# Channel mix's first buffers laid over attention's idle slots, its weights and first chunk prepared in attention's last groups, inverse sums by batch

## The reference

```python
x = x + attention(layernorm(x))          # 16 heads of 32, rotated q and k, softmax, then @ Wo + bo
# channel mix, on y = layernorm(x), y_prev = y one token earlier (zeros in front)
xr = mu_r * y + (1 - mu_r) * y_prev
xk = mu_k * y + (1 - mu_k) * y_prev
r = sigmoid(xr @ W_r.T)
k = square(relu(xk @ W_k.T))
x = x + r * (k @ W_v.T)
```

## Time and profile before

| | us |
|---|---|
| median of the runs | 3142.26 |
| lowest and highest run | 3140.79, 3144.47 |
| the profiled execution | 3138.19 |
| its span, first to last instruction | 3136.1 |
| TensorE busy | 3022.8 |
| GpSimd busy | 2093.0 |
| VectorE busy | 2239.5 |
| ScalarE busy | 1487.5 |

### The profile page before, as it was taken

The page is one execution under the profiler, slowest core; times in us unless marked ns, Lnnn a source line. Parts: engine busy times, 40 slices in busy tenths (PEclk is TensorE's granted clock), DMA queues, the critical chain, the costliest instruction groups (busy, mean ns, idle before and its releaser), DMA issues. The chain is left out here.

```text
span 3136.1 us, 42811 instructions
## 1 busy us (share of the span) xinstructions
PE 3022.8 (96%) x15468; PEld 2016.3 (64%) x15468; DVE 2239.5 (71%) x3351; ACT 1487.5 (47%) x2714; POOL 2093.0 (67%) x715
## 2 busy tenths in 40 slices
PE   7999999989999999999999999999967999999998
PEld 4888888855555555555555555555525777877776
DVE  4555556568777777777777777777628778678784
ACT  1222222226666666666666666666742223223232
POOL 0211112118999999999999999999944665666663
PEclk8999999989999999999999999999988999999999
DMA  3554545664656464655656464646243323313311
GB/s 105 173 183 167 177 168 177 188 152 107 137 115 145 99 146 107 139 119 126 132 123 140 108 145 98 149 109 135 52 125 87 108 62 99 107 54 107 107 54 41
DMA packets 188922, 381.78 MB, mean 122 GB/s; under 512 B 17088, under 2 KB 53088, under 8 KB 180704
## 3 DMA queue, kind: packets, MB, share of 16 engines
q1 hardware_dynamic: 179696, 313.70, 36.3%
q0 software_dynamic: 9072, 66.06, 10.3%
HBM read 194.59 MB, written 118.49 MB: 100 GB/s over the span
## 5 line engine op out<-in xcount | busy, mean ns | idle before, releaser
L278 DVE TENSOR_REDUCE part_max<-ps_m 128x1 f32<-128x512 f32 x1984 | 1213.8, 681 | 333.9 <-PE ps_m L262 333.0
L950 POOL TENSOR_TENSOR pairs<-probs 128x2048 f32<-128x2048 f32 x255 | 1179.8, 4632 | 144.6 <-ACT probs L923 131.8
L923 ACT ACTIVATE probs<-ps_s 128x512 f32<-128x512 f32 x2048 | 1036.6, 623 | 292.7 <-PE ps_s L815 276.8
L262 PE MATMUL ps_m<-k_stack,q_stack 96*128 96x512 f32 x1984 | 820.3, 415 | 15.0 <-DVE neg_max L275 8.2
L815 PE MATMUL ps_s<-q_stack,k_stack 97*128 97x512 f32 x2048 | 817.1, 402 | 5.6 <-PEq L311 3.6
L262 PEld LDWEIGHTS ps_m<-k_stack,q_stack 96*128 96x128 f32 x1984 | 376.7, 190 | 287.7 <-DVE part_max L278 136.7
L828 PE MATMUL ps_o<-probs,v_tiles 128*32 128x512 f32 x4096 | 495.6, 602 | 0.0
L815 PEld LDWEIGHTS ps_s<-q_stack,k_stack 97*128 97x128 f32 x2048 | 388.0, 190 | 130.0 <-ACT probs L923 21.2
L541 POOL TENSOR_TENSOR ln_rstd<-ln_rstd,ln_minus_half 128x4 f32<-128x4 f32 x16 | 16.1, 1009 | 415.9 <-DVE ln_rstd L584 415.9
L957 POOL TENSOR_TENSOR pairs<-pairs 128x2048 f32<-128x2048 f32 x63 | 288.4, 4578 | 4.9
L828 PEld LDWEIGHTS ps_o<-probs,v_tiles 128*32 128x32 f32 x4096 | 107.3, 109 | 234.5 <-issue 176.6
(11 more groups left out here) (180 smaller groups left out, 4809.8 us busy)
## 6 DMA issues: line engine op xcount, KB each, us to landing
pairs<-pairs POOLq DMA_DIRECT2D x63, 1024.0 KB, 8.5
q_stack<-q_hi_scratch SPq DMA_DIRECT2D x128, 256.0 KB, 6.2
k_stack<-k_hi_scratch SPq DMA_DIRECT2D x64, 512.0 KB, 10.7
x_in<-in_x SPq DMA_DIRECT2D x16, 1024.0 KB, 5.4
q_hi_scratch<-st_hi SPq DMA_DIRECT2D x64, 256.0 KB, 2.2
q_lo_scratch<-st_lo SPq DMA_DIRECT2D x64, 256.0 KB, 2.5
k_hi_scratch<-st_hi SPq DMA_DIRECT2D x64, 256.0 KB, 2.4
k_lo_scratch<-st_lo SPq DMA_DIRECT2D x64, 256.0 KB, 2.6
```

Of the source, the lines that this page charges most:

```text
L262: nc.tensor.matmul(bank[:, :], att["q"][r][0:ROWS, half, h, q * P:(q + 1) * P], att["k"][r][0:ROWS, h, kc * CH:(kc + 1) * CH], start=True, ...
L278: nc.vector.reduce_max(part_max[:, half, j, kc:kc + 1], bank[:, :], AX).then_inc(att["m_read"], 1)
L923: nc.scalar.activation(probs[:, (r * UNITS + u) % PR, x // HG, x % HG, :], ps_s[place(u * UT + x) % SR][:, :], ACT.Exp, scale=SCALE).then_ ...
L950: nc.gpsimd.tensor_tensor(pairs[:, w, :, :], probs[:, (r * UNITS + u) % PR, 0, :, :], probs[:, (r * UNITS + u) % PR, 1, :, :], ALU.add).th ...
```

## The change

- Attention's three slots keep their sizes, but the buffers of slots 0 and 2 are now laid over buffers that the mix keeps: in slot 0 `o_hi`, `o_lo`, `w_o`'s low part, `x_in`, `bo` and a quarter of `gate`; in slot 2 `w_o`'s high part, the low parts of w_k, w_r, w_v and `relu`. The raw weights are loaded to where their low parts will be made in place. `neg_max` has one half instead of two, with a wait on the copy of the other half before it is written.
- In group 30 SP loads w_k, w_r, w_v, mu_r and mu_k. In group 31 it loads w_o, the first chunk's outputs and inverse sums, bo and the first x. In the last group VectorE divides the chunk, and w_o and the chunk are split by ScalarE and VectorE; ScalarE's two casts stand before its last `take_o`.
- The sums of batch b are loaded in group 4b+5 (groups 5, 9 ... 29) directly after the loads of the group, inverted by VectorE in the middle of its 66 maxima steps, and stored at the end of the group. The last batch's are handled in the mix.
- The end of attention no longer waits for the landing of the last stores; SP waits for it at the start of the mix.
- In the mix GpSimd divides chunk 1 before `inv_std(0)`, with the inverse sums loaded into `ka_lo`; w_k and w_r are split first, w_v after the first normalise; TensorE waits for w_k's split before the first k product and for all before the first r product. The output of a chunk goes out by two DMAs.

```diff
@@ slots
-def group_buffers(att, sb, r):
+def slot_buffers(sb, r):
+    return (sb(f"q_stack{r}", [P, 2, FC, D], F32R), sb(f"k_stack{r}", [P, 2, FC, D], F32R), sb(f"v_tiles{r}", [P, KT, P]))
...
+def load_inverse(sp, mix, inv_d, dst, b, par):
+    cs = slice(par * CH, (par + 1) * CH)
+    inv_v = inv_d.rearrange("(b g a) t -> b g a t", g=FC, a=HG)
+    for a in range(HG):
+        sp.dma_start(dst[a * HD:(a + 1) * HD, :, :].bitcast(F32),
...
@@ max_reduce
-        if not is_first(m):
-            dve.wait_ge(att["m_stacked"][half], 16 * m)
-        nc.vector.tensor_scalar(neg_max[:, half, :], bank[0:HALF_TILES, 0:P], -1.0, None,
+        if half == 1 or not is_first(m):
+            dve.wait_ge(att["m_stacked"][1 - half], 16 * (m + half))
+        nc.vector.tensor_scalar(neg_max[:, :], bank[0:HALF_TILES, 0:P], -1.0, None,
@@ attend_block, SP
+        def BATCH_AT(n):
+            return n > FC and n % FC == 1
...
+            def batch_inverse(n):
+                for q in range(NQ):
+                    sp.wait_ge(l_stored[q], 16 * (n - 1))
+                sp.dma_start(l_batch[:], by_batch(l_s)[:, n // FC - 1:n // FC, :]).then_inc(mix["l_loaded"], 16)
...
             def step(i, r, n):
-                if not (type(n) is int and n + 2 >= NG):
-                    if not is_first(n):
-                        sp.wait_ge(pv_done, n * UNITS)
-                        sp.sem_inc(held, 1)
+                if not is_first(n):
+                    sp.wait_ge(pv_done, n * UNITS)
+                if n + 2 < NG:
                     load_group(sp, att, scratch, n + 2, (r + 2) % R3)
+                elif n + 2 == NG:
+                    weights_of_the_mix()
+                else:
+                    first_chunk_of_the_mix()
+                if BATCH_AT(n):
+                    batch_inverse(n)
...
-            for s in o_stored + l_stored:
-                sp.wait_ge(s, 16 * NG)
@@ attend_block, ACT, last group
                 if is_last(n):
+                    act.wait_ge(mix["w_loaded"]["o"], 16)
+                    nc.scalar.copy(mix["w_hi"]["o"], mix["w_raw"]["o"]).then_inc(mix["w_split_hi"], 1)
+                    act.wait_ge(mix["o_div"], 1)
+                    nc.scalar.copy(mix["o_hi"], mix["o_in"][:]).then_inc(mix["oh_done"], 1)
                     take_o(n, 1)
                     take_l(n, 1)
@@ attend_block, DVE
                     for u in range(USES):
+                        if BATCH_AT(n) and u == USES // 2:
+                            dve.wait_ge(mix["l_loaded"], 16 * (n // FC))
+                            if n // FC >= 2:
+                                dve.wait_ge(mix["inv_stored"], 16 * (n // FC - 1))
+                            nc.vector.reciprocal(inv_batch[:], l_batch[:]).then_inc(mix["inv_done"], 1)
                         max_reduce(nc, dve, att, ps_m, n + 1, u)
+                    return
+                dve.wait_ge(mix["o_loaded"], 16)
+                dve.wait_ge(mix["inv_loaded"], 16 * HG)
+                nc.vector.tensor_tensor(mix["o_in"][:], mix["o_in"][:], mix["o_lo"].bitcast(F32), ALU.mult).then_inc(mix["o_div"], 1)
+                dve.wait_ge(mix["w_split_hi"], 1)
+                nc.vector.tensor_tensor(mix["w_lo"]["o"], mix["w_raw"]["o"], mix["w_hi"]["o"], ALU.subtract).then_inc(mix["w_split_lo"], 1)
+                dve.wait_ge(mix["oh_done"], 1)
+                nc.vector.tensor_tensor(mix["o_lo"], mix["o_in"][:], mix["o_hi"], ALU.subtract).then_inc(mix["ol_done"], 1)
@@ mix_block, SP
+            for stored in mix["l_stored"] + mix["o_stored"]:
+                sp.wait_ge(stored, 16 * NG)
+            sp.dma_start(sums, by_batch(l_d)[:, B - 1:B, :]).then_inc(l_loaded, 16)
+            sp.wait_ge(ol_done, 1)
+            load_heads(sp, mix, o_d, 0, 1)
+            load_inverse(sp, mix, inv_d, first_inverse, 0, 1)
             sp.wait_ge(xb_done, TPC)
             sp.dma_start(x_in[:], x_v[0, 1]).then_inc(x_loaded, 16)
...
-                    sp.dma_start(out_v[i, par], gate[:]).then_inc(out_stored, 16)
+                    sp.dma_start(out_v[i, par, :, 0:TPC - 1, :], gate_most[:]).then_inc(out_stored, 16)
+                    sp.dma_start(out_v[i, par, :, TPC - 1, :], gate[TPC - 1]).then_inc(out_stored, 16)
@@ mix_block, ACT
-            weights_high("o")
-            o_high(0)
             for k in ORDER[1:]:
                 weights_high(k)
+            o_high(1)
             x_T(0, 0, 0)
-            o_high(1)
             highs(0)
@@ mix_block, GpSimd
             for s in range(TPC):
                 add_bias(0, 0, s)
+            divide(1)
             inv_std(0)
+            o_low(1)
             edge(0)
-            divide(1)
-            o_low(1)
@@ mix_block, DVE
-            dve.wait_ge(l_loaded, 16)
-            nc.vector.reciprocal(inv[:, 0:1, :], sums[:, 0:1, :]).then_inc(inv_done, 1)
-            weights_low(0)
...
+            weights_low(1)
+            weights_low(2)
+            dve.wait_ge(l_loaded, 16 * B)
+            nc.vector.reciprocal(inv, sums).then_inc(inv_done, 1)
             dve.wait_ge(small_loaded, 16 * 3)
-            for n in range(1, len(ORDER)):
-                weights_low(n)
             norm(0, 0)
-            nc.vector.reciprocal(inv[:, 1:B, :], sums[:, 1:B, :]).then_inc(inv_done, 1)
+            weights_low(3)
             shift(0, 0, 0)
```

More of the change, by code:

```diff
@@ new lines, in mix_buffers0, with mix_buffers2, raw_weights0 @@
+def mix_buffers0(sb):
+    return {"o_hi": sb("o_hi", [P, FC, CH], F32R), "o_lo": sb("o_lo", [P, FC, CH], F32R),
+            "w_o_lo": sb("mix_w_o_lo", [P, FC, D], F32R), "x_in": sb("mix_x_in", [P, TPC, D]),
+            "bo": sb("bo", [P, D]), "gate3": sb("gate3", [P, D])}
+def mix_buffers2(sb):
+    return {**{f"w_{k}": sb(f"mix_w_{k}", [P, FC, D], F32R) for k in ("o_hi", "k_lo", "r_lo", "v_lo")},
+            "relu": sb("relu", [P, 2, CH])}
+def raw_weights0(sb):
+    return [sb(f"raw_skip{i}", [P, FC, D]) for i in range(2)] + [sb("raw_o", [P, FC, D])]
@@ new lines, in raw_weights2, with mix_start @@
+def raw_weights2(sb):
+    return [sb("raw_skip2", [P, FC, D])] + [sb(f"raw_{k}", [P, FC, D]) for k in "krv"]
+def mix_start(buffers, raw, own, sem):
+    return {
+        **{k: buffers[k][:] for k in ("o_hi", "o_lo", "x_in", "bo", "gate3", "relu")},
+        "o_in": own("o_in", [P, FC, CH]),
+        "w_hi": {"o": buffers["w_o_hi"][:]},
+        "w_lo": {k: buffers[f"w_{k}_lo"][:] for k in "okrv"},
+        "w_raw": {k: a[:] for k, a in zip("okrv", raw)},
+        "mu_r": own("mu_r", [P, FC]), "mu_k": own("mu_k", [P, FC]),
+        "w_loaded": {k: sem(f"w_loaded_{k}") for k in "okrv"},
+        "small_loaded": sem("small_loaded"),
+        "x_loaded": sem("mix_x_loaded"), "o_loaded": sem("o_loaded"), "inv_loaded": sem("inv_loaded"),
+        "o_div": sem("o_div"), "oh_done": sem("oh_done"), "ol_done": sem("ol_done"),
+        "w_split_hi": sem("w_split_hi"), "w_split_lo": sem("w_split_lo"),
+        "l_loaded": sem("l_loaded"), "inv_done": sem("inv_done"), "inv_stored": sem("inv_stored"),
+        "o_stored": [sem(f"o_stored{q}") for q in range(NQ)],
+        "l_stored": [sem(f"l_stored{q}") for q in range(NQ)],
+    }
@@ L682, in _, with attend_block @@
             body(last_i, True)
-def attend_block(nc, sem, held, t, att, scratch, o_d, l_d):
+def attend_block(nc, sem, held, t, att, scratch, o_d, l_s, inv_d, slot2, mix, x_v, wo_d, wr_d, wk_d, wv_d, bo_d, mur_d, muk_d):
     KB = 2
@@ L745, in attend_block @@
         o_out = sem("o_out")
-        o_stored = [sem(f"o_stored{q}") for q in range(NQ)]
-        l_stored = [sem(f"l_stored{q}") for q in range(NQ)]
+        o_stored, l_stored = mix["o_stored"], mix["l_stored"]
         block = ctx.enter_context(nc.Block())
+        def BATCH_AT(n):
+            return n > FC and n % FC == 1
         def rounds(step):
@@ L993, in mix_block @@
         mixed = sb("mixed", [P, FC, CH])
-        xn = mixed[:].rearrange("p f t -> p (f t)").rearrange("p (s d) -> p s d", s=TPC)
+        relu = mix["relu"]
+        xn = mixed
         xk_hi = sb("xk_hi", [P, FC, CH], F32R)
@@ L998, in mix_block @@
         xr_lo = sb("xr_lo", [P, FC, CH], F32R)
-        relu = sb("relu", [P, RELU, CH])
         ka_hi = sb("ka_hi", [P, FC, CH], F32R)
         ka_lo = sb("ka_lo", [P, FC, CH], F32R)
-        gate = sb("gate", [P, TPC, D])
+        gate_most = sb("gate", [P, TPC - 1, D])
+        gate = [gate_most[:, s, :] for s in range(TPC - 1)] + [mix["gate3"]]
         stats = sb("mix_stats", [P, TPC, 6])
@@ L1193, in weights_high @@
                 act.wait_ge(w_loaded[k], 16)
-                nc.scalar.copy(w_hi[k][:], staging[k][:]).then_inc(w_split_hi, 1)
+                nc.scalar.copy(w_hi[k], mix["w_raw"][k]).then_inc(w_split_hi, 1)
             def o_high(c):
@@ L1275, in divide @@
                 pool.wait_ge(inv_loaded, 16 * HG * (c + 1))
-                nc.gpsimd.tensor_tensor(o_in[:], o_in[:], o_lo[:].bitcast(F32), ALU.mult).then_inc(o_div, 1)
```

(2 more changed lines are left out.)

179 lines of the change are left out of this document (86 added, 93 removed).

## The result

Seven runs of the changed kernel have a median of 3154.66 us (3151.5 to 3163.4), seven of the kernel before beside them 3144.29 (3140.79 to 3147.57). The ratio is 1.0039 (95% interval 1.0027 to 1.005): slower by 0.4%, where 3126 was forecast.

What follows compares the result with a forecast made beforehand. TensorE, busy for 96% of the span, was taken to bound the kernel. Profiled execution 3138.19 - 30.5 + 1.0 + 6.65 + 6.2 + 0.3 = 3121.8; the runs' median stands 4.1 above: 3126, range 3111 to 3140.

Steps and rivals of the forecast that it cites:

- The head of the mix: From attention's end to the first k product: chunk 0 prepared early, so that product starts sooner, 30.5 us gained.
- the shift, length: Start of the mix, diff to the end of xr_lo: 24.2 us falls to 15.9, as divide and o_low have passed.
- gain: First k product of the mix at 2360.2 against 2390.74: 30.5 us gained, bounds 25 and 35.
- both signs that the prediction asked for: Start of the mix: GpSimd's chunk 1 divide before the deviation, idle time ended by a load; normalise steps above 1.91 us.
- the 1.0 for that: Mix, after TensorE stands 4 us: products restart at the low clock, some 2 us, half taken as paid.
- the 0.3 for the extra output DMA: End of the kernel: output leaves by two DMAs a chunk, one issue more at the very end, 0.3 us.
- The reciprocals: Attention, mid-maxima of groups 5, 9 ... 29: seven reciprocals of 0.95 us go straight on to TensorE, 6.65 in all.
- Rival 3: Attention, mid-group: each reciprocal takes turns with GpSimd's pair sum, stalls of 24.9 us instead of 12.9, 3138; chance 0.07.
- at 0.5 behind v_tiles DVE waits ... = 6.2 us: Attention, mid-group: sums land 0.5 us behind v_tiles, so DVE's seven waits for them total 6.2 us.
- Rival 4: Attention: sums' load served only after v_tiles, at its own 4.8 us; waits 33.2, with reciprocals 39.9; 3153; chance 0.08.
- from a mean stall of 4.2 us a batch: Attention: mean stall a batch from which slower than before decides, against a net gain of 29.2 us at the seam.
- 12.9 forecast for attention: Attention's stalls in all: reciprocals 6.65 us and DVE's waits for the sums' load 6.2 us.

Runs made afterwards that it cites:

- experiment 6: Changed kernel with reciprocal and wait at step 49, plus: deviation before chunk 1's divide (3113.27 us, ratio 0.9907), or o_low held until chunk 0 is normalised (3107.15, 0.9881).
- the second experiment: Changed kernel with the batch sums' load issued ahead of the group's ten loads, reciprocal still in mid-group: 3119.9 us, ratio 0.9913.

## Why the prediction was wrong, step by step

**The head of the mix was right.** Counted from the end of attention's last product (2369.34 in after):

| | forecast | measured |
|---|---|---|
| project(0) starts | 1.5 | 2.2 |
| divide of chunk 1, from its first load's issue | 12.4 | 11.3 |
| chunk 0 normalised | 26.9 | 25.9 |
| last copy of xT | 31.4 | 30.2 |
| the shift, length | 15.9 | 16.3 |
| first k product | 48.1 | 47.3 |
| gain | 30.5 | 31.3 |

The divide stands before the deviation and its idle time is ended by a load; the normalise steps are longer than 1.91: both signs that the prediction asked for are there. As it had them, GpSimd's path and VectorE's are near a tie: VectorE's last step before the deviation (1.60 beside the divide, 0.17 without it in experiment 6) ends at 2387.99, GpSimd's divide at 2387.97. Its small terms were too fine to be judged. TensorE did restart k at the low clock (0.63 per product, as priced), but the rest of the mix took 744.65 for 745.36, so that neither the 1.0 for that nor the 0.3 for the extra output DMA shows; kernels that share this code had 740.7 to 749.8 there.

**The reciprocals were right** within a us: 6.65 forecast, 6.66 in all and 5.7 in mid-group by the second experiment. Rival 3, that they take turns with GpSimd, is out: in the stretch 974 to 978 above GpSimd is busy for all of its 4.00 us, and the reciprocal inside it takes 0.95. The normalise steps did take turns with it (6.09). The Trainium skill's rule (SBUF — State Buffer, "SBUF: two separate sides") allows for both: it has the pair held by VectorE operations in a two-port mode or with two SBUF inputs. On which side the reciprocal and these normalise steps are had to be read from a row.

**The step that failed is "at 0.5 behind v_tiles DVE waits ... = 6.2 us".** Two things were wrong in it.

- The landing. The sums land 2.0 to 5.6 us behind v_tiles, 3.4 in the mean, where 0.5 was put; v_tiles itself is only 0.5 later than before in the mean, though 2.4 in group 5 (18.1 for 15.7). They land 17.6 to 19.8 us from their issue in all seven, where DVE gives them 15.3 (955.91 to 971.2 in group 5). The prediction had read that DVE has no slack there, that the queue lands in order and that the next item lands 3.2 behind v_tiles, and put a small load near the front of that gap because it is small. But that item, the store of o, stood at the very place in the queue that the sums got, 0.5 to 0.7 us behind v_tiles' issue, and in the seven groups of the trace before it took 19.0, 20.0, 17.6, 18.9, 19.6, 19.3 and 19.6. Less 15.3 each that makes 26.9 of waiting: the sums, a quarter as large, landed as it had. 26.6 us of waiting for 6.2: 20.4 of the miss. Rival 4 had the better mechanism (served behind v_tiles) with 33.2, and 0.08 of the chance. That its 3153 lies beside the measured 3154.66 is luck: it had 39.9 for attention, where the traces have 50 to 52.
- The clock. A stall in mid-group was priced at its own length. The prediction had itself priced a fallen clock at the seam, after a hole of 4 us, and did not ask whether seven stalls of 2 to 5 us would do the same. They did: 18.7 us, the rest of the miss. It also moves rival 4's own point. That was to decide "from a mean stall of 4.2 us a batch", which is its 29.2 of the seam over seven, reciprocal and wait together. Measured are 3.8 + 0.95 = 4.75, so the sign would have turned even without the clock, but by only 33.3 - 31.3 = 2.0 us, which the runs would hardly show. The low clock makes a loss of it that they do.

Together: 12.9 forecast for attention + 20.4 + 18.7 = 52.0, against a seam of 31.3. These are the parts in the first pair of traces, 37 us more than forecast in all; the runs missed the forecast by 28.7.

The range (3111 to 3140) was too narrow for the same reason: its upper end took in the unknown landing only as a rival outside it, and had no term for what a stall does to the clock. A load that stands last in a queue of ten and is wanted within a microsecond of when they land deserved the larger part of the chance.

## What to carry to other kernels

Price a wait by what is queued behind it on its engine, and where that engine is in lockstep with the bottleneck, put the wait where the data have surely landed or the engine has a gap: here 16 steps later, or the load ten DMAs earlier, turned 0.4% slower into 1.2% or 0.9% faster. The small DMA had the landing time of the queue in front of it (19.5 us), not of its size (2.0 us), and whatever stood at that place in the trace before had the same one. And a stall on TensorE can cost more than its length: here 1.5 to 3.8 us again through the clock, at 2.7 us and longer every time, at 1.7 to 1.9 us in five of eight.

## What the runs showed of the hardware

- TensorE's clock reacts to single short stalls inside otherwise full work: 1.1 us left it at 1.00 in 7 of 7, 1.9 us dropped it in 4 of 7, one of 1.7 us dropped it too, 2.7 us did in 7 of 7. Each drop cost 1.5 to 3.8 us beyond the stall.
- A 64 KB load took 2.0 us (1.9 to 2.7) ahead of ten loads and 13.0 to 20.4 us behind them, whether or not a store followed; a 256 KB store at the same place took 17.6 to 20.0.
- A float32 reciprocal of 128 columns took 0.94 to 0.95 us beside a running GpSimd pass, while four normalise steps of 512 columns went from 1.91 to 6.09 beside one of 4.52.
